# A softmax tile that is turned through memory: one fetch per tile in place of four, 128-byte sends, and products that read the tile by steps

## The chip, the cores and the metric

The kernel runs on one core of one Trainium2 chip. The metric is the device time in microseconds (us) of one execution. The core has a matrix engine (TensorE, "PE" in the profile; its weight loads are "PEld"), VectorE ("DVE"), ScalarE ("ACT"), GpSimd ("POOL") and SyncE ("SP"), which here only issues transfers. Sixteen DMA engines carry them.

## The reference

Input x is 2 batches of 1024 tokens of width 512. One attention layer and one mixture of low-rank experts are added to it:

```
def _rmsnorm(t, w):
    return t * rsqrt(mean(t * t, axis=-1) + 1e-6) * w
q = rmsnorm((LN(x) @ Wq.T) as 32 heads of 128)      # LN: layer norm without weights
k = rmsnorm((LN(x) @ Wk.T) as 8 heads of 128);  v = (LN(x) @ Wv.T) as 8 heads of 128
scores = q . k / sqrt(128) + slope[head] * (key - query), masked where key > query
attn = softmax(scores);  out = attn @ v;  x = x + out @ Wo.T
x = x + 2 * sum_h gate_h(LN(x)) * (LN(x) @ A_h.T) @ B_h.T   # gate: 8 * softmax of 8 router logits
```

Everything is float32, with 4 query heads for each of the 8 key/value heads.

## The kernel before

**Tiling.** Work goes by `w`, 16 windows: window w is one key/value head (8 of them, `NG`) of one batch. In a window the 1024 queries are 8 tiles `s` of 128 rows, the keys 8 tiles `j` of 128, and because of the mask only tiles j <= s are computed. `G = 4` query heads go together. For each (w, s): four `scores` products into PSUM (one per head h), `max` on DVE (which also moves the scores into `probs`), `exp` on ACT, `invert` on DVE, `normalise` on POOL, one instruction for each head over a row of (s+1)*128 keys. Then, for every j, the 128x128 probability blocks of the four heads have to be turned, so that keys lie on partitions, and `values` multiplies them with v into `o_ps` (128 x 512: four heads by 128 queries). `y` multiplies the result by the output weights.

**Precision.** A float32 operand is split in a high and a low part (type fp32r), and each product is three matmuls (high*high, high*low, low*high) in `split_product`; all of them have line L1106 in the profile. So one `values` is three matmuls of 128 x 512.

**Two ways to turn a tile.** A table `MEMORY_TILES` says by stage and s which j go through memory (`through_memory`). The others (260 of 576) are turned on PE: `turn.p`, four transposes, then `high` on ACT and `low` on DVE. The 316 tiles that go through memory take this way:
- `send_p` (SP, L642): once for each head, the head's normalised rows of all memory tiles of this s go to `p_bounce` in DRAM. It waits for `normalise` of that head.
- `fetch_p` (SP, L653): it waits until all four heads have landed and until the raw tile's last user (`lower_p`, L887) is done, then issues four transfers, one for each block of 32 keys. Each brings for 32 partitions sixteen pieces of 32 floats (128 bytes) for each partition. The four counts are added up in one semaphore, `p_fetched`.
- `flip_p` (DVE, L987): a transpose of every 32 x 32 block, in place. Now keys lie on partitions, and the 512 columns are (head, query).
- `upper_p` (ACT, L797) and `lower_p` (POOL, L887) split the tile in `pT_hi` and `pT_lo` (also `_a` and `_b`, further slots of early and late windows; raw tiles `p_raw`, `p_raw_b` likewise).
- `values` (PE) multiplies it, after the tiles of the same s that were turned on PE.

**Order.** The order of the work on every engine is written out by hand in the plans (`PROLOGUE`, `GROUP_A`, `BOUNDARY`, `FIRST_B`, `GROUP_B`, `LAST`); every engine takes its own items from them in order, and an item that waits holds up all that is behind it on its engine. SP's queue holds the sends, the fetches, loads of x and stores. The windows 0 to 6 are stage 0, window 7 is stage 1, and the windows 8 to 15 are stage 2. Weights are loaded, spilled and read back by transfers issued from ACT.

Of the kernel before, what the change touches and what calls it, by code (L numbers as in the profile page):

```python
# [11 lines left out]
F32 = mybir.dt.float32  # L12
# [3 lines left out]
P = 128  # L16
# [291 lines left out]
def attention_lora_block(nc, x, Wq, Wk, Wv, Wo, q_norm_w, k_norm_w, A, B, Wr, br, out):  # L308
# [4 lines left out]
    G = H // NG  # L313
    NE, RK, _ = A.shape
    NT = S // P
# [12 lines left out]
    BLOCK = 32  # L328
    NBLK = P // BLOCK
# [10 lines left out]
    def stage(w):  # L340

        return 0 if w < NG - 1 else 1 if w < NG else 2

    def through_memory(w, s):

        return list(MEMORY_TILES[stage(w)].get(s, ()))
# [4 lines left out]
    def ffn_batch(w):  # L351
        return 0 if w < LAST_W else 1
# [39 lines left out]
    raw_tile, raw_uses, raw_before = {}, {}, {}  # L392
# [41 lines left out]
    with ExitStack() as ctx:  # L434
        def sb(name, shape, dt=F32):
            return ctx.enter_context(nc.sbuf_tensor(name, shape, dt))

        def psum(name, shape):
            return ctx.enter_context(nc.psum_tensor(name, shape, F32))

        def sem(name):
            return ctx.enter_context(nc.semaphore(name))
# [12 lines left out]
        v_hi = sb("v_hi", [P, NT, HD], F32R)  # L455
        v_lo = sb("v_lo", [P, NT, HD], F32R)
        kv_raw = sb("kv_raw", [P, NT, 2 * HD])
        rel = sb("rel", [P, S])
        probs = [sb("probs_even", [P, G, S - P]), sb("probs_odd", [P, G, S])]
# [66 lines left out]
        def p_high(slot):  # L526
            return turned_pairs[slot][0]

        def p_low(slot):
            return turned_pairs[slot][1]  # L530

        def raw_p(n):
            return raws[n]


        early = [name for name in p_slot if name[0] < NG - 1]
        last_early_slots = [[name for name in early if p_slot[name] == TURN_SLOTS + MEMORY_SLOTS + i][-1] for i in range(MORE_SLOTS[0])]
# [2 lines left out]
        def ffn_place_free(engine):  # L540
            for name in last_early_slots:
                after(engine, "values", *name)
            for name in last_early_raws:
                after(engine, "lower_p", *name)

        def x_source(b, t):
            if b == 0:
                return y[:, t, :]
            return w_raw[:, (t + G) % (G + 2), :]
# [14 lines left out]
        def pairs(turned):  # L564
            return turned[:].rearrange("p (a c) n -> p a (c n)", c=2).bitcast(F32)

        p_bounce = nc.dram_tensor("p_bounce", [2, NT, G, P, P], F32).ap()

        s_ps = psum("s_ps", [P, 1024])
        turn_ps = [psum(f"turn_ps{i}", [P, 512]) for i in range(RING)]  # L570
# [1 line left out]
        o_ps = psum("o_ps", [P, 512])  # L572
# [4 lines left out]
        p_sent = [sem("p_sent_even"), sem("p_sent_odd")]  # L577
        p_fetched = [sem(f"p_fetched{i}") for i in range(RAW_TILES + sum(MORE_RAW))]
# [25 lines left out]
        def after(engine, kind, *key):  # L604
            engine.wait_ge(sems[kind], number[(kind, *key)])
# [6 lines left out]
        @block.sync  # L612
        def _(sp):
            x_v = x.rearrange("b (t p) d -> b p t d", p=P)
            out_v = out.rearrange("b (t p) d -> b p t d", p=P)

            def load_wkv(w, *first):
                if first:
                    sp.dma_start(w_raw[:, G, :], wk_v[0]).then_inc(wkv_loaded, 16)
                    sp.dma_start(w_raw[:, G + 1, :], wv_v[0]).then_inc(wkv_loaded, 16)  # L620

            def load_wq(w, *first):
                if first:
                    sp.dma_start(w_raw[:, 0:G, :], wq_v[0]).then_inc(wq_loaded, 16)

            def load_wo(w, *first):
                if first:

                    sp.dma_start(wk_norm[:], k_norm_w.rearrange("(p a) -> p a", a=1)).then_inc(small_loaded, 16)
                    sp.dma_start(wq_norm[:], q_norm_w.rearrange("(p a) -> p a", a=1)).then_inc(small_loaded, 16)  # L630
                    sp.dma_start(br_row[:], br.rearrange("(a n) -> a n", a=1).broadcast_to((P, NE))).then_inc(small_loaded, 16)
                    after(sp, "turn", "wq", 0, C - 1)
                    sp.dma_start(w_raw[:, 0:G, :], wo_v[0]).then_inc(wo_loaded, 16)

            def send_p(w, s, h):

                first = through_memory(w, s)[0]
                before = [name for name in sent if name[1] % 2 == s % 2 and sent[name] == sent[w, s] - 16 * G]
                if before and h == 0:
                    after(sp, "flip_p", *before[0], through_memory(*before[0])[-1])  # L640
                after(sp, "normalise", w, s, h)
                sp.dma_start(p_bounce[s % 2, first:s + 1, h].rearrange("u p c -> p u c"),  # L642
                             probs[s % 2][:, h, first * P:(s + 1) * P].rearrange("p (u c) -> p u c", c=P)).then_inc(p_sent[s % 2], 16)

            def fetch_p(w, s, j):

                n = raw_tile[w, s, j]
                sp.wait_ge(p_sent[s % 2], sent[w, s])
                if raw_before[w, s, j]:
                    after(sp, "lower_p", *raw_before[w, s, j])  # L650
                blocks = p_bounce[s % 2, j].rearrange("h (a i) (b j) -> b i (h a) j", i=BLOCK, j=BLOCK)
                for b in range(NBLK):
                    sp.dma_start(raw_p(n)[b * BLOCK:(b + 1) * BLOCK, :].rearrange("p (n j) -> p n j", j=BLOCK),  # L653
                                 blocks[b]).then_inc(p_fetched[n], 16)

            def load_y(w, t):
                b = 0 if w < 0 else 1
                if b:
                    sp.wait_ge(stored[t], 16)
                sp.dma_start(y[:, t, :], x_v[b, :, t, :]).then_inc(y_loaded[t], 16)  # L660

            def load_x(w, t):
                if t < 2:
                    after(sp, "turn", "wkv", NG - 1, 1)
                elif t < G + 2:
                    after(sp, "turn", "wo", NG - 1, G - 1)
                else:
                    after(sp, "turn", "x", 1, t - G - 2)
                sp.dma_start(x_source(1, t), x_v[1, :, t, :]).then_inc(x_loaded[t], 16)

            def load_a(w):
                ffn_place_free(sp)
                sp.dma_start(f_x[:, 0, :], A.rearrange("h r d -> (h r) d")).then_inc(a_loaded, 16)

            def load_wr(w):
                ffn_place_free(sp)
                sp.dma_start(f_x[0:NE, 1, :], Wr).then_inc(wr_loaded, 16)

            def load_b(w):
                after(sp, "turn", "a")  # L680
                sp.dma_start(b_raw, B.rearrange("h (p o) r -> p h o r", o=C)).then_inc(b_loaded, 16)

            def store(w, t):
                b = ffn_batch(w)
                after(sp, "add_f", b, t)
                sp.dma_start(out_v[b, :, t, :], y[:, t, :]).then_inc(stored[t], 16)

            follow({"load_wkv": load_wkv, "load_wq": load_wq, "load_wo": load_wo, "send_p": send_p, "fetch_p": fetch_p, "load_y": load_y,
                    "load_x": load_x, "load_a": load_a, "load_wr": load_wr, "load_b": load_b, "store": store})
            for t in range(NT):  # L690
                sp.wait_ge(stored[t], 16 * NB)
# [200 lines left out]
        def _(dve):  # L892
# [89 lines left out]
                                                   ALU.subtract).then_inc(sems["low"], 1)  # L982

            def flip_p(w, s, j):
                dve.wait_ge(p_fetched[raw_tile[w, s, j]], 16 * NBLK * raw_uses[w, s, j])
                raw = raw_p(raw_tile[w, s, j])
                nc.vector.transpose(raw, raw).then_inc(sems["flip_p"], 1)  # L987

# [105 lines left out]
        def _(pe):  # L1094
# [8 lines left out]
            def split_product(target, pairs, start=True, stop=True):  # L1103
                for i, ((a_hi, a_lo), (b_hi, b_lo)) in enumerate(pairs):
                    for k, (a, m) in enumerate(((a_hi, b_hi), (a_hi, b_lo), (a_lo, b_hi))):
                        last = nc.tensor.matmul(target, a, m, start=start and i == 0 and k == 0,  # L1106
                                                stop=stop and i == len(pairs) - 1 and k == 2)
                return last
# [124 lines left out]
            def values(w, s, j):  # L1233
                order = values_order(w, s)
                if j == order[0]:
                    if s == 0:
                        after(pe, "v_low", w)
                    if w or s:
                        after(pe, "o_low", w - (s == 0), (s - 1) % NT)
                r = p_slot[w, s, j]  # L1240
                if j in through_memory(w, s):
                    after(pe, "lower_p", w, s, j)
                else:
                    after(pe, "low", "p", w, s, j)
                split_product(o_ps[:], [((v_hi[:, j, :], v_lo[:, j, :]), (p_high(r), p_low(r)))],
                              start=j == order[0], stop=j == order[-1]).then_inc(sems["values"], 1)

            def y_product(w, s):
# [42 lines left out]
```

## Time and profile before

| | |
|---|---|
| median of 3 runs | 2059.68 us (2056.29 to 2061.45) |
| the profiled execution's own time | 2058.6 us |
| its span | 2056.5 us |
| PE busy | 1993.2 us, 97% |
| DVE, POOL, ACT busy | 1363.5, 1189.2, 1162.6 us |
| DMA engines, SP's queue | 41.7% of 16 engines' span |
| tiles fetched through memory | 316, by 1264 transfers of 64 KB |
| sends | 384, of 64 to 384 KB |

The span runs from the first to the last instruction; the run's own time is 2.1 us longer. Busy time of PE is the union of its matmuls, whose modelled lengths overlap: two matmuls that start 0.23 us apart may each be listed at 0.39 us. So the distance between starts, and not the listed length, is the price of a matmul in a full stream.

### The profile page before, as it was taken

How to read it: one execution, taken by the hardware profiler on the slowest of the kernel's cores; microseconds unless marked ns; L12 is line 12 of the kernel's file. 1: busy time of each engine (PE TensorE's matmuls, PEld its weight loads, DVE VectorE, ACT ScalarE, POOL GpSimd, SP SyncE). 2: the span in 40 equal slices, each digit the busy share in tenths (PEclk: the TensorE clock that was granted, in tenths of full speed). 3: DMA queues.
4: the chain of work that ended last, by engine and by line, in shares of the span. 5: the costliest groups of instructions: out<-in, count | busy, mean ns of one | idle time of the engine just before them, and what ended most of it. 6: DMA issues, size and time to landing. Idle time of an engine off the chain costs nothing.

```text
span 2056.5 us, 33589 instructions
## 1 busy us (share of the span) xinstructions
PE 1993.2 (97%) x10956; PEld 1698.1 (83%) x10956; DVE 1363.5 (66%) x3431; ACT 1162.6 (57%) x3314; POOL 1189.2 (58%) x1188
## 2 busy tenths in 40 slices
PE   7999999999999999999999899999999999999996
PEld 6888888888888888888888788787878878788774
DVE  6667667666666666768876566565666656566696
ACT  4656656565665656655555465555656555465552
POOL 3574645647465574655645557465664746657473
PEclk9999999999999999999999999999999999999998
DMA  4573855657466573765635637365463745637254
GB/s 164 138 161 119 192 141 150 132 154 166 129 171 145 136 159 113 181 181 142 135 109 141 142 96 173 96 154 139 123 124 108 172 101 137 161 81 165 69 122 99
DMA packets 896141, 283.81 MB, mean 138 GB/s; under 512 B 677721, under 2 KB 839513, under 8 KB 895969
## 3 DMA queue, kind: packets, MB, share of 16 engines
q1 hardware_dynamic: 844064, 179.44, 41.7%
q10 hardware_dynamic: 51904, 102.24, 14.2%
q8 instruction: 88, 1.44, 0.3%
q14 instruction: 85, 0.69, 0.1%
HBM read 152.59 MB, written 128.97 MB: 137 GB/s over the span
## 4 chain that ended last, share of the span: by engine, by line
PE 76%; SPq 8%; DMA 4%; DVE 4%; issue 4%; POOL 2%; ACT 2%; DVEq 0%; POOLq 0%; ACTq 0%
PE s_ps L1106 16%; PE q_ps L1106 15%; PE y_ps L1106 14%; PE o_ps L1106 14%; PE turn_ps L1193 9%; SPq L653 7%; PE turn_ps L1106 7%; DMA p_bounce<-probs_odd 2%; POOL probs_odd L881 1%; DMA p_raw_b<-p_bounce 1%; DMA p_bounce<-probs_even 1%; DVE oT_lo L1029 1%; PE turn_ps L1187 1%; SPq L642 1%; ACT oT_hi L823 1%
## 5 line engine op out<-in xcount | busy, mean ns | idle before, releaser
L881 POOL TENSOR_TENSOR probs_odd<-probs_odd,p_inv 128x256 f32<-128x256 f32 (+3 forms) x256 | 318.0, 1257 | 180.1 <-DVE p_inv L1008 179.2
L881 POOL TENSOR_TENSOR probs_even<-probs_even,p_inv 128x128 f32<-128x128 f32 (+3 forms) x256 | 261.3, 1043 | 191.3 <-DVE p_inv L1008 190.5
L1106 PE MATMUL s_ps<-kT_hi,qT_hi 128*128 128x512 f32 (+3 forms) x768 | 272.5, 355 | 4.1 <-DVE neg_max L1001 3.8
L1001 DVE CUSTOM_DVE_ANT_0 probs_odd<-s_ps,rel 128x256 f32<-128x256 f32 (+3 forms) x256 | 209.3, 820 | 97.3 <-issue 96.6
L802 ACT ACTIVATE probs_odd<-probs_odd,neg_max 128x256 f32<-128x256 f32 (+3 forms) x256 | 212.2, 831 | 91.7 <-DVE neg_max L1001 91.6
L1106 PE MATMUL s_ps<-kT_hi,qT_lo 128*128 128x512 f32 (+3 forms) x768 | 262.4, 342 | 0.0
L1106 PE MATMUL s_ps<-kT_lo,qT_hi 128*128 128x512 f32 (+3 forms) x768 | 261.7, 341 | 0.0
L802 ACT ACTIVATE probs_even<-probs_even,neg_max 128x128 f32<-128x128 f32 (+3 forms) x256 | 185.1, 725 | 118.7 <-DVE neg_max L1001 118.4
L1001 DVE CUSTOM_DVE_ANT_0 probs_even<-s_ps,rel 128x128 f32<-128x128 f32 (+3 forms) x256 | 174.9, 687 | 109.8 <-issue 108.8
L987 DVE STREAM_TRANSPOSE p_raw<-p_raw 128x512 f32<-128x512 f32 x252 | 174.9, 700 | 83.5 <-DMA p_raw<-p_bounce 83.2
L1106 PE MATMUL q_ps<-wqT_hi,xnT_hi 128*128 128x512 f32 x512 | 217.2, 424 | 1.0 <-DVE qn L1012 0.8
L1106 PE MATMUL y_ps<-woT_hi,oT_hi 128*128 128x512 f32 x512 | 204.8, 400 | 10.9 <-DVE oT_lo L1029 8.6
L789 ACT ACTIVATE pT_hi<-turn_ps 128x512 fp32r<-128x512 f32 x260 | 154.3, 597 | 107.3 <-PE turn_ps L1193 107.3
L887 POOL TENSOR_TENSOR pT_lo<-p_raw,pT_hi 128x512 fp32r<-128x512 f32 x134 | 173.8, 1301 | 49.7 <-ACT pT_hi L797 49.6
L1106 PE MATMUL q_ps<-wqT_hi,xnT_lo 128*128 128x512 f32 x512 | 201.6, 394 | 0.0
L1106 PE MATMUL y_ps<-woT_hi,oT_lo 128*128 128x512 f32 x512 | 200.5, 392 | 0.0
L1106 PE MATMUL q_ps<-wqT_lo,xnT_hi 128*128 128x512 f32 x512 | 200.4, 391 | 0.0
L1106 PE MATMUL y_ps<-woT_lo,oT_hi 128*128 128x512 f32 x512 | 199.9, 390 | 0.0
L979 DVE TENSOR_TENSOR pT_lo<-turn_ps,pT_hi 128x512 fp32r<-128x512 f32 x260 | 174.8, 677 | 27.2 <-ACT pT_hi L789 26.1
L811 ACT ACTIVATE qn<-q_ps 128x128 f32<-128x128 f32 x512 | 134.7, 280 | 94.9 <-PE q_ps L1106 93.9
L1106 PE MATMUL o_ps<-pT_hi,v_hi 128*128 128x512 f32 x426 | 177.3, 416 | 4.5 <-DVE pT_lo L979 3.7
L1106 PEld LDWEIGHTS s_ps<-kT_hi,qT_hi 128*128 128x128 f32 x768 | 144.6, 188 | 32.0 <-DVE neg_max L1001 9.1
(131 smaller groups left out, 5068.3 us busy)
## 6 DMA issues: line engine op xcount, KB each, us to landing
p_raw<-p_bounce SPq DMA_DIRECT2D x1008, 64.0 KB, 2.3
p_bounce<-probs_odd SPq DMA_DIRECT2D x60, 384.0 KB, 3.1
p_raw_b<-p_bounce SPq DMA_DIRECT2D x256, 64.0 KB, 2.4
p_bounce<-probs_odd SPq DMA_DIRECT2D x60, 256.0 KB, 2.8
p_bounce<-probs_even SPq DMA_DIRECT2D x60, 256.0 KB, 3.0
p_bounce<-probs_even SPq DMA_DIRECT2D x64, 192.0 KB, 2.4
wq_kept<-wqT_hi ACTq DMA_DIRECT2D x8, 1024.0 KB, 4.5
wq_kept<-wqT_lo ACTq DMA_DIRECT2D x8, 1024.0 KB, 6.8
```

The costliest lines, as they stand in the source:

```text
L642: sp.dma_start(p_bounce[s % 2, first:s + 1, h].rearrange("u p c -> p u c"), probs[s % 2][:, h, first * P:(s + 1) * P].rearrange("p (u c) - ...
L653: sp.dma_start(raw_p(n)[b * BLOCK:(b + 1) * BLOCK, :].rearrange("p (n j) -> p n j", j=BLOCK), blocks[b]).then_inc(p_fetched[n], 16)
L789: nc.scalar.activation(target, bank, ACT.Copy).then_inc(sems["high"], 1)
L802: nc.scalar.activation(row, row, ACT.Exp, bias=neg_max[:, s % 2, h:h + 1], scale=-1.0, accum_out=p_sum[:, s % 2, h:h + 1]).then_inc(sems[" ...
L811: last = nc.scalar.activation(qn[:, h, :], q_ps[:, h * HD:(h + 1) * HD], ACT.Square, scale=float(slopes[gg % NG * G + h]), accum_out=q_sum ...
L881: nc.gpsimd.tensor_tensor(row, row, p_inv[:, s % 2, h:h + 1].to_broadcast((P, L)), ALU.mult).then_inc(sems["normalise"], 1)
L887: nc.gpsimd.tensor_tensor(p_low(r), raw_p(raw_tile[w, s, j]), p_high(r).bitcast(F32), ALU.subtract).then_inc(sems["lower_p"], 1)
L979: nc.vector.tensor_tensor(target, bank, upper.bitcast(F32), ALU.subtract).then_inc(sems["low"], 1)
L987: nc.vector.transpose(raw, raw).then_inc(sems["flip_p"], 1)
L1001: nc.vector.tensor_tensor_reduce(out=probs[s % 2][:, h, 0:L], in0=s_ps[:, at_col:at_col + L], in1=rel[:, S - L:S], scale=-float(slopes[w % ...
L1106: last = nc.tensor.matmul(target, a, m, start=start and i == 0 and k == 0, stop=stop and i == len(pairs) - 1 and k == 2)
L1193: last = nc.tensor.transpose(bank[0:width, i * rows:(i + 1) * rows], source, ident[0:rows, 0:rows])
```

## The change

In memory, a tile is now laid out as `[head, j, block of 32 keys, query row, 32 keys]`. A send writes pieces of 32 floats (128 bytes) in place of 128 floats (512 bytes). A fetch is one transfer for all 128 partitions: partition (b, i) takes, for each head, the four query rows 4i to 4i+3 of key block b, which lie together (512 bytes). So row q is split as q = 4i + a, and not as q = 32a + i as before. After `flip_p` the columns of the tile are in the order (head, a, i), and `values` reads the tile with a step of 32 floats over a, inside steps of 1 over i, so that the product's columns come out in the order of the queries. Tiles turned on PE are read as before. `flip_p`, `upper_p` and `lower_p` work on the same 128 x 512 tiles, and all plans are the same.

```
+        def rows_in_order(tile):
+            return tile.rearrange("p (h a i) -> p h i a", h=G, a=NBLK)
...
-        p_bounce = nc.dram_tensor("p_bounce", [2, NT, G, P, P], F32).ap()
+        p_bounce = nc.dram_tensor("p_bounce", [2, G, NT, NBLK, P, BLOCK], F32).ap()
...
-                sp.dma_start(p_bounce[s % 2, first:s + 1, h].rearrange("u p c -> p u c"),
-                             probs[s % 2][:, h, first * P:(s + 1) * P].rearrange("p (u c) -> p u c", c=P)).then_inc(p_sent[s % 2], 16)
+                sp.dma_start(p_bounce[s % 2, h, first:s + 1].rearrange("u b p j -> p (u b) j"),
+                             probs[s % 2][:, h, first * P:(s + 1) * P].rearrange("p (u j) -> p u j", j=BLOCK)).then_inc(p_sent[s % 2], 16)
...
-                blocks = p_bounce[s % 2, j].rearrange("h (a i) (b j) -> b i (h a) j", i=BLOCK, j=BLOCK)
-                for b in range(NBLK):
-                    sp.dma_start(raw_p(n)[b * BLOCK:(b + 1) * BLOCK, :].rearrange("p (n j) -> p n j", j=BLOCK),
-                                 blocks[b]).then_inc(p_fetched[n], 16)
+                tile = p_bounce[s % 2, :, j].rearrange("h b (i a) j -> (b i) h (a j)", a=NBLK)
+                sp.dma_start(raw_p(n).rearrange("p (h k) -> p h k", h=G), tile).then_inc(p_fetched[n], 16)
...
-                dve.wait_ge(p_fetched[raw_tile[w, s, j]], 16 * NBLK * raw_uses[w, s, j])
+                dve.wait_ge(p_fetched[raw_tile[w, s, j]], 16 * raw_uses[w, s, j])
...
+                target, upper, lower = o_ps[:], p_high(r), p_low(r)
                 if j in through_memory(w, s):
                     after(pe, "lower_p", w, s, j)
+
+                    target = target.rearrange("p (h i a) -> p h i a", h=G, a=NBLK)
+                    upper, lower = rows_in_order(upper), rows_in_order(lower)
                 else:
                     after(pe, "low", "p", w, s, j)
-                split_product(o_ps[:], [((v_hi[:, j, :], v_lo[:, j, :]), (p_high(r), p_low(r)))],
+                split_product(target, [((v_hi[:, j, :], v_lo[:, j, :]), (upper, lower))],
                               start=j == order[0], stop=j == order[-1]).then_inc(sems["values"], 1)
```

## Rows read from the trace of the kernel before

**Rows 1.** The page: engines' busy time, and the DMA queue of SP.

```profile
PE 1993.2 (97%) x10956; PEld 1698.1 (83%) x10956; DVE 1363.5 (66%) x3431; ACT 1162.6 (57%) x3314; POOL 1189.2 (58%) x1188
...
q1 hardware_dynamic: 844064, 179.44, 41.7%
```

**Rows 2.** Windows: us, busy us of PE, PEld, DVE, ACT, POOL, clock, DMA share, GB/s.

```profile
0.00:16.00 16.00, 5.58 (x28) 4.81 (x28) 11.01 (x64) 4.91 (x8) 7.08 (x20) 1.00 0.68 230
16.00:1108.00 1092.00, 1082.01 (x6084) 929.91 (x6085) 749.32 (x1870) 642.19 (x1842) 621.99 (x632) 1.00 0.58 146
...
1856.00:2056.50 200.50, 179.70 (x908) 143.33 (x906) 142.05 (x351) 93.38 (x249) 113.11 (x110) 0.97 0.49 108
```

**Rows 3.** Waits of PE: us in total, times, longest us.

```profile
PE turn_ps L1193 <- DVE probs_odd L917: 10.1, 1, 10.1
PE o_ps L1106 <- POOL pT_lo_b L887: 9.5, 13, 1.8
```

**Rows 4.** Timeline of PE in window 9: start us, us, engine, instruction.

```profile
1393.75 0.28 PE L1106 MATMUL turn_ps<-wkvT_hi,xnT_hi 128*128 128x256 f32 x1
...
1395.18 0.28 PE L1106 MATMUL turn_ps<-wkvT_hi,xnT_hi 128*128 128x256 f32 x1
...
1403.50 0.40 PE L1106 MATMUL o_ps<-pT_hi_b,v_lo 128*128 128x512 f32 x1
...
1404.89 0.39 PE L1106 MATMUL o_ps<-pT_hi,v_lo 128*128 128x512 f32 x1
```

**Rows 5.** Copies on DVE at L944: duration ns min/median/max, starts, shape.

```profile
L944 DVE COPY f_x<-turn_ps x16: 645/682/692, 950.2 to 2045.3; 128x512 f32<-128x512 f32 x16
...
L944 DVE COPY low_turned<-turn_ps x16: 251/281/293, 967.0 to 2050.9; 128x128 f32<-128x128 f32 x16
...
L944 DVE COPY bT<-turn_ps x1: 1076/1076/1076, 944.3 to 944.3; 128x512 f32<-128x512 f32 x1
```

**Rows 6.** Issues of sends and fetches on SP's queue: issue ns min/median/max.

```profile
L653 SPq DMA_DIRECT2D p_raw<-p_bounce x1008: 302/488/2642, 67.4 to 2023.9; - x168
L653 SPq DMA_DIRECT2D p_raw_b<-p_bounce x256: 302/488/2061, 1101.2 to 2028.1; - x128
L642 SPq DMA_DIRECT2D p_bounce<-probs_even x192: 319/376/1095, 59.6 to 1993.7; - x192
```

**Rows 7.** DMA issues of the page: KB each, median us to landing.

```profile
p_raw<-p_bounce SPq DMA_DIRECT2D x1008, 64.0 KB, 2.3
p_bounce<-probs_odd SPq DMA_DIRECT2D x60, 384.0 KB, 3.1
...
p_bounce<-probs_odd SPq DMA_DIRECT2D x60, 256.0 KB, 2.8
...
p_bounce<-probs_even SPq DMA_DIRECT2D x64, 64.0 KB, 1.5
```

**Rows 8.** Timeline of SP's queue, fetches of s = 7 in window 9.

```profile
1402.82 6.29 SPq L653 DMA_DIRECT2D p_raw<-p_bounce  x12
```

**Rows 9.** DMA queue in 1402 to 1413, fetches alone: packets, MB, share.

```profile
q1 hardware_dynamic: 10781, 1.34, 76.8%
```

**Rows 10.** DMA queue in 1398 to 1400, sends alone.

```profile
q1 hardware_dynamic: 1202, 0.60, 103.2%
```

**Rows 11.** Waits of DVE and of SP's queue for those transfers: us, times, longest.

```profile
DVE p_raw L987 <- DMA p_raw<-p_bounce: 83.2, 63, 4.2
DVE p_raw_b L987 <- DMA p_raw_b<-p_bounce: 41.7, 27, 3.4
...
SPq L653 <- DMA p_bounce<-probs_odd: 116.1, 41, 8.9
SPq L653 <- DMA p_bounce<-probs_even: 112.6, 40, 8.4
```

**Rows 12.** Timeline of PE at the fifth tile of that s, with the idle time before.

```profile
1416.31 0.50 PE L1106 MATMUL o_ps<-pT_hi_b,v_hi 128*128 128x512 f32 x1 [0.87 <-POOL pT_lo_b L887]
```

**Rows 13.** Normalisation on POOL by row length: count, busy us, mean ns of one.

```profile
L881 POOL TENSOR_TENSOR probs_odd<-probs_odd,p_inv 128x1024 f32<-128x1024 f32 x64 | 121.0, 1902 | 31.2 <-DVE p_inv L1008 31.2
```

## The prediction

> **What bounds the kernel now.** I read the page's busy times first: PE is busy for 1993.2 of 2056.5 us, and no other engine for more than 1363.5 [rows 1]. Then the windows, to see where PE's 63.3 idle us lie: 10.4 in the first 16 us, 20.8 in the last 200, and only 10 in the 1092 us of the windows 0 to 7 [rows 2]. The rest, some 22 us, lies in the later windows. The granted clock is 1.00 in the full stretches, the upper of its two levels, so PE has nothing to gain there. Then PE's waits: the largest is at the start, 10.1 us, and the next, 9.5 us in 13 cases, is of `values` for `lower_p`, that is, for a tile that comes through memory [rows 3]. So the kernel is bound by PE's stream. What shortens the road through memory can return about 10 us directly; what makes a matmul longer is paid in full.
>
> The chain of waits of the page goes through SP for 8% and DMA for 4%, which looks like more. But a chain only tells the order of releases: PE was at work on other items while those transfers ran, and 3% idle is the ceiling of any gain.
>
> **What one stepped product costs.** The change makes 316 tiles times three matmuls = 948 matmuls read their moving operand by steps. In a full stream six matmuls of 512 columns start within 1404.89 - 1403.50 = 1.39 us, 0.232 each, and twelve of 256 columns within 1.43 us, 0.119 each [rows 4]. The difference, 0.1125 us for 256 columns, gives 0.225 us for the columns of one product, beside 0.007 of fixed price. So a column comes at full pace, and a slower read cannot hide behind the fixed part.
>
> No matmul of this trace reads by steps, so the price has to be bounded. Below: nothing, if reading by 128-byte steps is as fast as reading in a row. Above, the nearest row is on another engine and for a write: the one copy that goes to SBUF by steps of 16 bytes, `bT`, takes 1076 ns where the copies of the same size take 682 and those of 128 columns 281 [rows 5]. From 682 and 281, a contiguous element costs 401/384 = 1.04 ns and the fixed part is 148 ns; then a stepped one costs (1076 - 148)/512 = 1.81 ns, 1.74 times as much. Carried to PE as a ratio this is 0.74 x 0.225 = 0.167 us for each matmul, 948 x 0.167 = 158 us. Carried as a rate (an element each 1.81 ns) it is 0.928 - 0.225 = 0.70 us, 666 us in all. I take a factor of two, 0.225 x 948 = 213 us: if an array that takes a column at every step of its clock misses its operand, it loses a whole step at the least, and two is the first whole number above 1.74. It is an estimate from rows 4 and 5, and nearer to the ratio than to the rate, since one copy of DVE says more on how much a missed line costs an engine than on how fast PE's own port is.
>
> The Trainium skill has a rule that speaks against the change: "SBUF — State Buffer", section "Door 1: The DMA port swizzle (why `[64,N]` ≈ `[32,N]`)", says that SBUF is read in lines of 16 bytes, that a pattern needs two hits in a line for full bandwidth, and that each crossing to a new line pays. With steps of 128 bytes every element is in another line than the one before it. The `bT` copy agrees with it in kind, on a write and on DVE [rows 5]; no row here shows it for PE. The page gives no figure, so the sum above stands as it is.
>
> Nothing else changes on PE: the number of matmuls, weight loads and PSUM columns is the same, and the output is written in order.
>
> **The fetch.** A fetch is four issues of 488 ns at the median [rows 6]; in a stream of them twelve take 6.29 us, 0.524 each, so a tile costs SP 2.10 us [rows 8]. After it is one issue. Is an issue of more pieces longer? The sends have 128 to 768 pieces, and they are issued in 376 ns at the median, less than a fetch of 512 [rows 6]; I take 0.5 us a tile. DMA work: in the stretch with fetches alone 10781 packets take 76.8% of 16 engines for 11 us, 12.5 ns each [rows 9]; with sends alone 1202 take 103.2% for 2 us, 27.5 ns each [rows 10]. A tile is 2048 pieces of 128 bytes before, 1.60 us, and 512 of 512 bytes after, 0.88 us. So six tiles in a row (s = 7) come in about 5.3 us where they took 12.6. One transfer of 512 such pieces, 256 KB, lands in about 2.8 us, as the send of that size does [rows 7]; now the fourth of a tile's transfers is issued 1.6 us after the first and lands 2.3 later. The first tile gains 1.1 us.
>
> **The send.** Its pieces go from 512 to 128 bytes and are four times as many: 3072 for one head at s = 7. Their packet as a write to memory is in no row; from below I price it as the read of 128 bytes, 12.5 ns, from above as the 512-byte packet, 27.5 ns, and take the lower, since the two rows fit a price that goes by the bytes (one stretch reads memory, the other writes it, and neither stands out) [rows 9, 10]. The number of 128-byte packets stays 316 x 2048 = 647 thousand; they only move from fetch to send. A head takes 2.4 us where it took 1.32. POOL hands over a head each 1.90 us [rows 13], so three heads build up 3 x 0.5 us, and the last lands 1.5 + 1.1 = 2.6 us later. Queued behind it on SP are the fetches, which wait for all four heads (228.7 us of such waits in 81 cases) [rows 11]; behind the fetch `flip_p` on DVE, then ACT, POOL and `values`. At s = 7 the first tile is so late by 2.6 - 1.1 = 1.5 us, and the sixth early by 7.3 - 2.6 = 4.7.
>
> That sixth is where it counts: the stream of tiles is what PE waits for there, 0.87 us before the fifth [rows 12], while the first tile stands behind two tiles that were turned on PE. DVE also stands less in `flip_p`, where it now waits 124.9 us in 90 cases [rows 11]. What PE can get back is its own waits: 9.5 us [rows 3], perhaps as much again out of waits behind a delayed DVE. I take -10 us, between 0 and -25. The same 10 us fall away if PE is slowed instead, as its producers then have more time: they are counted once.
>
> **The sum** for the likeliest case, against the profiled execution's own 2058.6 us: 2058.6 + 213 - 10 = 2262 us. That execution is 1 us under the median of the runs, 2059.68, which changes nothing.
>
> **The rivals.**
> - *The stepped read is free* (the other sign). Place: the 948 matmuls of `values`. For it: the steps are regular, and only the order of addresses changes. Against: `bT` [rows 5]. Then what is left is the shorter road: 2058.6 - 10 = 2049 us, 2034 to 2059 by the bounds. It decides below a price of 10/948 = 0.011 us for a matmul, 5% of its columns.
> - *The read is far slower*, at the rate of `bT`, 1.81 ns an element: 2058.6 + 666 - 10 = 2715 us. For it: if the price is a latency of the memory and not of the engine, it is the same time for everyone. Against: DVE's contiguous element takes 1.04 ns, PE's 0.44, so the two ports have not the same pace to begin with.
> - *The sends become the bound*, with a free read. At 27.5 ns a piece a head of s = 7 takes 5.3 us against POOL's 1.90; the last lands 3 x 3.4 + 4.0 = 14 us later, and the fetches give back 7.3. At s = 5 and 6 (four tiles) it is some 3 us each after what the fetches give back. That is 13 us a window, 208 us over 16 windows, of which I take half to be covered by other PE work: 2058.6 + 104 = 2163 us. It starts to lose at 4 x (192 p - 1.9) = 7.3 us, p = 19 ns a packet. The Trainium skill, "DMA: Bandwidth & Descriptors", section "Specifications", says that below 512 bytes the engine does a read-modify-write; no row here shows it for a write, and the 128-byte reads of rows 9 show no such price.
> - *The change does not do what it says*: a transfer of 128-byte pieces might hold SP for longer, so that the three issues saved come back in the sends. Against it is that issue time does not grow with the pieces [rows 6]. With it the gain is gone, and nothing more: 2059 with a free read.
>
> **How the numbers follow.** Read slowed about twofold, 2262 (own range 2206 to 2290: the ratio of 1.74 without more, and the factor two with nothing gained): 0.45. Read free: 0.33, of which 0.20 is faster by over 0.3% (6 us, about what a measurement of this kernel can tell from no change) and 0.13 within it. Far slower: 0.12. Sends the bound: 0.05. The rest, 0.05, is some small loss of another kind. The range goes from 2040, which takes in most of the free case, to 2300; it leaves out the far slower read and a few of the others, 0.19. Faster 0.20, same 0.14, slower 0.66.
>
> **What the profile of the changed kernel would show.** If I am right, the matmuls of `values` come in two kinds: those of tiles turned on PE start 0.23 us apart, those of fetched ones about 0.45; PE's busy time grows by some 200 us, `flip_p` no longer waits for DMA, and PE's wait for `pT_lo_b` is gone. If both kinds start 0.23 apart, the read is free, and the result is decided on the road through memory: by the landing time of the sends (2.5 to 3.1 us now at 256 to 384 KB; I expect about 5 at 384 KB), and by SP's queue at s = 7, one issue a tile. A landing of over 10 us would be the rival of the sends. Wrong the forecast would be above all if the moving operand's port does not care for lines.

## The result and the profile after

The changed kernel is slower by 0.6%: 2070.52 us (median of 4 runs, 2069.65 to 2071.27) against 2058.27 us of the kernel before, ratio 1.0062, 95% interval 1.0049 to 1.0074. I had forecast slower, and 2262 us: right in sign and in the direction of the mechanism, but 203 us of loss where 12 came, because one term, the price of the stepped read, was five times too large.

The page of the kernel after, with the lines that answer to [rows 1] and [rows 7]:

```profile
span 2069.2 us, 32641 instructions
...
PE 2024.2 (98%) x10956; PEld 1701.7 (82%) x10956; DVE 1356.6 (66%) x3431; ACT 1162.1 (56%) x3314; POOL 1193.7 (58%) x1188
...
q1 hardware_dynamic: 828896, 179.38, 43.3%
...
p_raw<-p_bounce SPq DMA_DIRECT2D x252, 256.0 KB, 3.3
p_bounce<-probs_odd SPq DMA_DIRECT2D x60, 384.0 KB, 4.8
```

PE is busy for 31.0 us more (2024.2 against 1993.2) and idle for 45.0 us in place of 63.3. So PE's own work grew by more than the whole loss, and some of its waits are gone. A fetch is one transfer, in the air for 3.3 us; a send of 384 KB lands after 4.8 us where it took 3.1.

The timeline of PE after, in window 9 (start us, us, instruction), to be read beside [rows 4]:

```profile
1417.12 0.39 PE L1107 MATMUL o_ps<-pT_hi,v_lo 128*128 128x512 f32 x1
1417.35 0.39 PE L1107 MATMUL o_ps<-pT_hi,v_hi 128*128 128x512 f32 x1
1417.58 0.39 PE L1107 MATMUL o_ps<-pT_lo,v_hi 128*128 128x512 f32 x1
1417.80 0.39 PE L1107 MATMUL o_ps<-pT_hi,v_lo 128*128 128x512 f32 x1
1418.03 0.43 PE L1107 MATMUL o_ps<-pT_hi_b,v_hi 128*128 128x512 f32 x1
1418.30 0.43 PE L1107 MATMUL o_ps<-pT_lo_b,v_hi 128*128 128x512 f32 x1
1418.57 0.43 PE L1107 MATMUL o_ps<-pT_hi_b,v_lo 128*128 128x512 f32 x1
```

The first four belong to tiles turned on PE and start 0.23 us apart. The last three read a fetched tile by steps and start 0.27 apart. So there are two kinds, as forecast, but the step costs 0.27 - 0.23 = 0.04 us and not 0.225; over 948 matmuls some 40 us and not 213. (The listed lengths overlap, so it is the distance between starts that counts.)

The waits of PE after (us in total, times, longest):

```profile
PE turn_ps L1194 <- DVE probs_odd L918: 10.0, 1, 10.0
...
PE y_ps L1107 <- DVE oT_lo L1030: 4.5, 8, 0.7
...
PE o_ps L1107 <- DVE pT_lo L980: 0.5, 1, 0.5
```

The 9.5 us for `pT_lo_b` of [rows 3] have no successor: no product waits any longer for a fetched tile. DVE's waits for fetched tiles fell from 124.9 us [rows 11] to 49.9; I had expected them to be gone:

```profile
DVE p_raw L988 <- DMA p_raw<-p_bounce: 39.7, 30, 3.4
...
DVE p_raw_b L988 <- DMA p_raw_b<-p_bounce: 10.2, 8, 2.0
```

### The profile page after: what moved, and what is told of

Same layout as the page of the kernel before. It is cut to its first block, busy times and chain, and to the rows that moved or that the text cites. A ratio compares the mean times of both kernels' runs of the same rounds, so it can differ in the third digit from the quotient of the medians.

```text
span 2069.2 us, 32641 instructions
## 1 busy us (share of the span) xinstructions
PE 2024.2 (98%) x10956; PEld 1701.7 (82%) x10956; DVE 1356.6 (66%) x3431; ACT 1162.1 (56%) x3314; POOL 1193.7 (58%) x1188
## 4 chain that ended last, share of the span: by engine, by line
PE 92%; DVE 3%; issue 1%; ACT 1%; POOL 1%; DMA 1%; SPq 0%; DVEq 0%; POOLq 0%; ACTq 0%
PE o_ps L1107 20%; PE s_ps L1107 18%; PE y_ps L1107 17%; PE q_ps L1107 17%; PE turn_ps L1194 11%; PE turn_ps L1107 8%; PE turn_ps L1188 1%; PE y_ps L1271 0%; DVE qn L1013 0%; DVE oT_lo L1030 0%; DMA p_raw_b<-p_bounce 0%; ACT oT_hi L824 0%; DVE y L1036 0%; ACT qn L812 0%; DMA y<-in_L_attn_x 0%
## 5 line engine op out<-in xcount | busy, mean ns | idle before, releaser
L1107 PE MATMUL o_ps<-pT_hi,v_hi 128*128 128x512 f32 x426 | 183.7, 431 | 0.8 <-DVE pT_lo L980 0.5
L1107 PE MATMUL o_ps<-pT_hi,v_lo 128*128 128x512 f32 x426 | 174.6, 410 | 0.0
```

## The experiments

**The two halves by themselves.** The theory after the result: the stepped read costs some 40 us (A), and the shorter road gives part of it back. The rival (B): the loss is the sends' small pieces. First the read alone, in the kernel before:

```
 # the kernel before, and in values (rows_in_order as in the change):
+                target, upper, lower = o_ps[:], p_high(r), p_low(r)
...
+                    target = target.rearrange("p (h i a) -> p h i a", h=G, a=NBLK)
+                    upper, lower = rows_in_order(upper), rows_in_order(lower)
```

> The kernel before, its memory layout, sends and fetches untouched; only the 948 products of fetched tiles read the turned tile by the steps of the change. (The columns of the four heads come out in another query order, so the values of the output differ.) Theory A, the loss of the change is the price of the stepped read and the shorter road gives part of it back: these matmuls start 0.27 us apart in place of 0.23, PE's busy time grows by some 40 us, and the time is 2058 + 41 less what PE's waits for producers give back (up to 13): 2085 to 2100 us, clearly above the 2070.5 of the whole change. Theory B, the stepped read costs little where producers are late anyway, and the loss comes from the sends of 128-byte pieces: 2058 to 2065 us.

Measured: 2080.66 us against 2056.66, ratio 1.0114 (1.0101 to 1.0128), 24.0 us slower. It came out just below the range, and far above what B allows. By form, the products of fetched tiles before and, below them, in that run (count, busy us, mean ns of one):

```profile
L1106 PE MATMUL o_ps<-pT_lo_b,v_hi 128*128 128x512 f32 x80 | 31.7, 396 | 0.0
...
L1106 PE MATMUL o_ps<-pT_lo_a,v_hi 128*128 128x512 f32 x70 | 27.6, 395 | 0.0
```

```profile
L1109 PE MATMUL o_ps<-pT_lo_b,v_hi 128*128 128x512 f32 x80 | 35.0, 438 | 0.0
...
L1109 PE MATMUL o_ps<-pT_lo_a,v_hi 128*128 128x512 f32 x70 | 30.5, 436 | 0.0
```

Each is 0.041 to 0.042 us longer, some 40 us for 948. Of these, 24 reach the end: most of the rest falls into time in which PE stood idle anyway (63.3 us before, 50.0 here). Then the road alone, the whole change with the read put back:

```
 # the kernel after, and in values:
-                    target = target.rearrange("p (h i a) -> p h i a", h=G, a=NBLK)
-                    upper, lower = rows_in_order(upper), rows_in_order(lower)
```

> The whole change, but the products read the fetched tiles in a row. (The columns are then in another query order, so the values of the output differ.) Theory A: the road through memory is faster than before, PE gets back its waits for fetched tiles, and the time falls below before: 2030 to 2052 us, with PE busy time as before, 1993. Theory B, the small pieces of the sends are the loss: 2062 to 2070 us, with PE waiting for pT_lo more than the 9.5 us of before.

Measured: 2039.91 us, ratio 0.9918 (0.9904 to 0.9931), 16.7 us faster. A is right, B falls. The two halves add up to +7.3 us, the whole change was +12.3: with the shorter road there is less idle time left for the slower products to hide in. PE's idle time shows it: the read alone takes 13.3 us of the 63.3 away, the road alone 14.2 (49.1 are left), and both together only 18.3 (45.0 are left). They are two effects of opposite sign, of which the change keeps the difference.

**What on the road gives the gain.** Four transfers of 512-byte pieces in place of one, in the improved kernel told below (2038 us), so the pieces of sends and fetches are the same in both:

```
 # the kernel with two stored identities, and in fetch_p:
-                tile = p_bounce[s % 2, :, j].rearrange("h b (i a) j -> (b i) h (a j)", a=NBLK)
-                sp.dma_start(raw_p(n).rearrange("p (h k) -> p h k", h=G), tile).then_inc(p_fetched[n], 16)
+                for b in range(NBLK):
+                    tile = p_bounce[s % 2, :, j, b].rearrange("h (i a) j -> i h (a j)", a=NBLK)
+                    sp.dma_start(raw_p(n)[b * BLOCK:(b + 1) * BLOCK, :].rearrange("p (h k) -> p h k", h=G),
+                                 tile).then_inc(p_fetched[n], 16)
```

> The run with two identity tiles, but a tile is again fetched by four transfers of 32 partitions each, now of 512-byte pieces (the sends stay at 128 bytes). The output is the reference's. Theory A: the gain on the road through memory is that of SP's queue (2.1 us a tile by four issues of 0.52): with four issues back, the time returns from 2038 to about 2055 or above, since the sends still land 1 to 1.7 us later. Theory B: it is the DMA engines' work (0.9 us a tile in place of 1.6), and four issues of larger pieces keep most of it: 2038 to 2045 us.

Measured: 2106.70 us, ratio 1.0247 (1.023 to 1.0263). It went A's way, but no theory saw the size: the three further issues of a tile cost 68 us, and bring the kernel 50 us over the kernel before, which has as many. SP's queue at s = 7 of window 9, with four issues and with one:

```profile
1424.10 1.75 SPq L664 DMA_DIRECT2D p_raw_b<-p_bounce  x4
1425.94 5.59 SPq L664 DMA_DIRECT2D p_raw<-p_bounce  x12
1431.64 3.71 SPq L664 DMA_DIRECT2D p_raw_b<-p_bounce  x8
```

```profile
1394.82 0.36 SPq L663 DMA_DIRECT2D p_raw_b<-p_bounce  x1
1395.28 1.55 SPq L663 DMA_DIRECT2D p_raw<-p_bounce  x3
1397.17 4.11 SPq L663 DMA_DIRECT2D p_raw_b<-p_bounce  x2
```

24 issues take 11.3 us, six take 6.5. Of the six, five go out within 3.1 us, and the last stands 3.0 us for its raw tile, which `lower_p` still reads. The pieces of a fetch are larger than before, and yet with four issues SP needs 0.47 us for each (0.52 before [rows 8]): a tile is then paced by the issues, not by the bytes. The late sends (4.2 us to landing at 384 KB, where the kernel before has 3.1), which one issue a tile pays for, are here without cover. DVE stands in `flip_p` for 184.3 us where the kernel before has 124.9 [rows 11], and PE waits for DVE's other work behind it (waits of DVE and of PE in the run with four issues):

```profile
DVE p_raw L1003 <- DMA p_raw<-p_bounce: 121.2, 82, 4.8
...
DVE p_raw_b L1003 <- DMA p_raw_b<-p_bounce: 63.1, 28, 4.4
...
PE o_ps L1122 <- DVE pT_lo L995: 20.4, 7, 5.3
PE y_ps L1122 <- DVE oT_lo L1045: 15.0, 14, 2.7
```

Behind them the clock falls as well; window of the same run: PE busy for 9.79 of 12 us, granted clock 0.86. Over the whole run the granted clock is 0.989 in place of 0.997, and PE's busy time 17.5 us above that of the kernel before.

```profile
1424.00:1436.00 12.00, 9.79 (x40) 7.65 (x39) 6.25 (x9) 4.09 (x7) 5.32 (x4) 0.86 0.44 125
```

So with four issues a tile the new layout (sends in 128-byte pieces, fetches in 512-byte ones) loses some 50 us against the old one, the fallen clock included. Of its two sides the fetches land sooner (2.0 us in place of 2.3) and the sends later, so I put the loss on the sends; small sends with the old fetches were not run. What the change gives by one issue in place of four is 68, in this kernel and with these sends.

**Why the step is cheap.** I had expected a factor of two. Three probes on the kernel before, each with another order of reading the fetched tiles; nothing else differs:

```
 p1: tile.rearrange("p (h i a) -> p h a i", h=G, a=4)   # steps of 4 floats, runs of 32
 p2: tile.rearrange("p (x y a) -> p y x a", a=4, x=8)   # 4 floats in a row, then 64 on
 p3: tile.rearrange("p (h i a) -> p h a i", h=G, a=2)   # steps of 2 floats, runs of 64
```

> The kernel before; the products of fetched tiles read steps of 4 floats (16 bytes) in runs of 32. (Columns in another order, so the output's values differ.) If the price is for each element in another 16-byte line, these matmuls are as slow as with steps of 32 floats, 0.437 us each by the profile, against 0.396 in a row. If it is for each restart of the inner run (128 restarts with steps of 32, 16 here), about 0.401. If it is for the distance of 128 bytes, 0.396.

> The kernel before; the products of fetched tiles read runs of 4 floats in a row (16 bytes), each run 32 floats behind the one before it. (Columns in another order, so the output's values differ.) Price for elements in another line: a run is one line, as in a row, 0.396 us. Price for restarts: 128 as in the change, 0.437 us.

> The kernel before; the products of fetched tiles read steps of 2 floats (8 bytes) in runs of 64, two elements for each line of 16 bytes. (Columns in another order, so the output's values differ.) If two elements a line are enough for full pace, 0.396 us; if the price grows with the lines for each element, half of the price of 16-byte steps, about 0.41; if for restarts (8 of them), 0.398.

(In p2 the next run starts 64 floats further on, and not 32 as its expectation says: with x = 8, y has 16 values, and a step of x is 16 x 4 floats. It has 128 runs of 4 all the same.)

Measured, one execution each: 2247.14, 2082.64 and 2238.81 us. The middle one costs about what the change's order costs. The other two cost a factor of two for each product, and come within 15 and 23 us of the 2262 that I had forecast. Three consecutive starts of p1, p2 and p3, from their timelines of PE:

```profile
1420.14 0.66 PE L1109 MATMUL o_ps<-pT_hi_b,v_hi 128*128 128x512 f32 x1
1420.60 0.66 PE L1109 MATMUL o_ps<-pT_lo_b,v_hi 128*128 128x512 f32 x1
1421.06 0.66 PE L1109 MATMUL o_ps<-pT_hi_b,v_lo 128*128 128x512 f32 x1
```

```profile
1424.18 0.44 PE L1109 MATMUL o_ps<-pT_hi_b,v_hi 128*128 128x512 f32 x1
1424.45 0.45 PE L1109 MATMUL o_ps<-pT_lo_b,v_hi 128*128 128x512 f32 x1
1424.73 0.46 PE L1109 MATMUL o_ps<-pT_hi_b,v_lo 128*128 128x512 f32 x1
```

```profile
1494.42 0.63 PE L1109 MATMUL o_ps<-pT_lo_b,v_hi 128*128 128x512 f32 x1
1494.87 0.63 PE L1109 MATMUL o_ps<-pT_hi_b,v_lo 128*128 128x512 f32 x1
1495.33 0.63 PE L1109 MATMUL o_ps<-pT_hi,v_hi 128*128 128x512 f32 x1
```

0.46, 0.27 to 0.28 and 0.45 us apart. For p1 and p3 all theories fall: none allowed more than 0.04 us over a read in a row, and these take 0.22 and more. A price for each element in another line falls also because the change's own order changes line with every element, too, and costs 0.27. Only for p2 did a theory's number come, that of the 128 restarts. So what was open is why the change's order is cheap and p1's is not: the distance of 128 bytes, the short run of 4, or that the change returns to the same four lines with the next run. Three more probes tell these apart:

```
 q1: tile.rearrange("p (g a y) -> p g y a", a=4, y=4)   # steps of 4, runs of 4, each line again after 4 columns
 q2: tile.rearrange("p (a i) -> p i a", a=16)           # steps of 32, runs of 16, each line again after 16
 q3: tile.rearrange("p (a x y) -> p y x a", a=4, y=4)   # steps of 128, runs of 4, each line again after 128
```

> The kernel before; the products of fetched tiles read steps of 4 floats in runs of 4, four such runs within 16 floats, so that every 16-byte line is touched again after three others. (Columns in another order, so the output's values differ.) If what makes the change's read cheap is the distance of 128 bytes, this one costs what steps of 4 floats in runs of 32 did: 0.46 us from start to start. If it is the short run, or that a line is touched again soon, 0.27.

> The kernel before; the products of fetched tiles read steps of 32 floats in one run of 16 over the whole tile, then the next column. (Columns in another order, so the output's values differ.) Distance decides: 0.24 to 0.27 us, with 32 restarts in place of 128. The short run or an early return to the same line decides: 0.46.

> The kernel before; the products of fetched tiles read steps of 128 floats in runs of 4, and the next run starts 4 floats on, so that no 16-byte line is touched again before 128 columns. (Columns in another order, so the output's values differ.) If the run of 4 alone makes the read cheap: 0.27 us. If it is the early return to the same lines: 0.46.

Measured, one execution each: 2079.78, 2222.71 and 2270.69 us. Starts of q1, q2 and q3:

```profile
1421.37 0.43 PE L1109 MATMUL o_ps<-pT_hi_b,v_hi 128*128 128x512 f32 x1
1421.63 0.43 PE L1109 MATMUL o_ps<-pT_lo_b,v_hi 128*128 128x512 f32 x1
1421.90 0.43 PE L1109 MATMUL o_ps<-pT_hi_b,v_lo 128*128 128x512 f32 x1
```

```profile
1500.45 0.61 PE L1109 MATMUL o_ps<-pT_lo_b,v_hi 128*128 128x512 f32 x1
1500.88 0.61 PE L1109 MATMUL o_ps<-pT_hi_b,v_lo 128*128 128x512 f32 x1
1501.31 0.61 PE L1109 MATMUL o_ps<-pT_hi_b,v_hi 128*128 128x512 f32 x1
```

```profile
1416.73 0.65 PE L1109 MATMUL o_ps<-pT_hi_b,v_hi 128*128 128x512 f32 x1
1417.20 0.67 PE L1109 MATMUL o_ps<-pT_lo_b,v_hi 128*128 128x512 f32 x1
1417.69 0.66 PE L1109 MATMUL o_ps<-pT_hi_b,v_lo 128*128 128x512 f32 x1
```

0.27, 0.43 and 0.48 us. Distance is not it: 16 bytes (q1) is as cheap as 128. A short run is not it: q3 has runs of 4 and is the dearest. The theory of the early return said what each of the three would do before they ran, and all three came out about so. It holds in all seven orders: where four neighbouring floats (16 bytes, called a line here) are used one after the other or with a return after 4 columns (the change, p2, q1), a matmul costs 0.27 to 0.28; where a part of a line is used now and another 16 or more columns later (q2, q3, p1, and p3, which uses two floats at a time), 0.43 to 0.48. A return after 5 to 15 columns was not tried. That such lines are held for a moment is inferred from these seven; how many, and for how long, was not tried.

Two things stay open. The first is the size of the line. p3 uses two floats of each 16 bytes in succession, so it changes line half as often as p1, and yet costs as much (0.45 against 0.46). With a unit of 8 bytes it would use one float of each at a time, as p1 does, and all seven orders would fit as well; pairs of floats in a row, with jumps between them, would decide and were not run. The second is the 0.04 us itself. The early return tells the cheap orders from the dear ones, but not a cheap one from a read in a row: p2 uses each line whole and at once, and still pays it. The three cheap orders have 128 short runs each, so a small price for each restart, 0.3 ns, would give it; a price for each jump does not fit, since the change jumps 512 times and p2 128 times. Cheap orders with fewer or more restarts were not run.

**Where else the step can be put.** The two engines that split the tile can put its rows in order:

```
-                nc.scalar.activation(p_high(...), raw_p(...), ACT.Copy)
+                nc.scalar.activation(in_rows(p_high(...)), rows_in_order(raw_p(...)), ACT.Copy)
...
-                nc.gpsimd.tensor_tensor(p_low(r), raw_p(...), p_high(r).bitcast(F32), ALU.subtract)
+                nc.gpsimd.tensor_tensor(in_rows(p_low(r)), rows_in_order(raw_p(...)), in_rows(p_high(r)).bitcast(F32), ALU.subtract)
```

> The whole change, but the order of the rows is put right one step earlier: upper_p on ScalarE and lower_p on GpSimd read the raw tile by the steps of 32 floats and write in a row, and the products read in a row. The output is the reference's. Theory A, a stepped read costs any engine something, and here it falls on engines that are busy for 56 to 58%: upper_p goes from 0.63 to 0.7 to 1.3 us, lower_p from 1.3 to at most 2.6; if it is under 0.3 us each it is hidden and the time is that of the run with the road alone, 2030 to 2052; at a doubling, lower_p holds GpSimd for another 400 us in the windows where it is already the pace of the last tiles, and the time is 2070 to 2150. Theory B (the sends are the loss): not below 2062 in any case.

Measured: 2064.10 us, ratio 1.0037 (1.0025 to 1.005). Better than the change, not better than before, and between A's two ranges. B's "not below 2062" is met too; it is the run with the road alone that excludes B, not this one. The two instructions, before and in this run (count, busy us, mean ns of one):

```profile
L887 POOL TENSOR_TENSOR pT_lo<-p_raw,pT_hi 128x512 fp32r<-128x512 f32 x134 | 173.8, 1301 | 49.7 <-ACT pT_hi L797 49.6
...
L797 ACT ACTIVATE pT_hi<-p_raw 128x512 fp32r<-128x512 f32 x134 | 84.1, 628 | 59.5 <-DVE p_raw L987 55.1 <-PE o_ps L1106 4.1
```

```profile
L891 POOL TENSOR_TENSOR pT_lo<-p_raw,pT_hi 128x512 fp32r<-128x512 f32 x134 | 213.1, 1597 | 51.6 <-ACT pT_hi L801 51.1
...
L801 ACT ACTIVATE pT_hi<-p_raw 128x512 fp32r<-128x512 f32 x134 | 156.2, 1172 | 49.1 <-DVE p_raw L991 47.0
```

The same order of reading that costs PE 18% costs ScalarE 87%: it falls on the chain from the landed tile to the product, 0.54 + 0.30 us a tile, and this run is 24 us above the road alone. PE waits 11.9 us here for the low parts that POOL makes, and not at all in the run with the road alone.

**No step at all.** If partition 4i+a of the scores holds query 32a+i, the fetched tile comes out in the natural order by itself. A turn on PE should permute for nothing if the identity that it multiplies with has its columns permuted; the mask table is permuted once, through memory:

```
+        eye_p = sb("eye_p", [P, P])    # ident, read "p (i a) -> p a i" once
...
-                    last = nc.tensor.transpose(bank[...], source, ident[0:rows, 0:rows])
+                    eye = eye_p[:] if of == "p" else ident[:].rearrange("p (a i) -> p i a", a=NBLK) if of == "q" else ident[0:rows, 0:rows]
+                    last = nc.tensor.transpose(bank[...], source, eye)
...
+                    sp.dma_start(rel_kept, rel[:]).then_inc(rel_sent, 16)
+                    sp.wait_ge(rel_sent, 16)
+                    sp.dma_start(rel[:], rel_kept.rearrange("(a i) n -> i a n", a=NBLK)).then_inc(rel_back, 16)
```

> The whole change with no stepped product at all and the reference's output: the query tile is turned against an identity whose columns are permuted, so that partition 4i+a of the scores holds query 32a+i, the mask table is permuted alike through memory once at the start, and tiles turned on TensorE use the inverse permuted identity. The only stepped reads left are the 512 of the small query turns (128 columns each). Theory A: the time of the road alone plus at most 5 us: 2033 to 2055, below before. Theory B: 2062 to 2072.

Measured: 2095.29 us, ratio 1.0189 (1.0175 to 1.0203), 40 us above A's range and 23 above B's. Its timeline of PE has the reason: four turns with the stored identity, and four that read it by steps.

```profile
1217.70 0.60 PE L1208 MATMUL turn_ps<-eye_p,probs_even 128*128 128x128 f32 x4
1218.83 1.05 PE L1208 MATMUL turn_ps<-ident,qn 128*128 128x128 f32 x4
```

0.45 us more for four turns, 0.11 each, over 512 turns 58 us. I had allowed 5, from the price in `values`. These are turns of plain float32, not of fp32r, and there the same order of reading (steps of 32 floats, runs of 4) doubles the time, from 0.11 to 0.22 us from start to start. With a second stored identity, for which keeping one `low_gated` tile in place of two makes room:

```
-        eye_p = sb("eye_p", [P, P])
+        eyes = {"p": sb("eye_p", [P, P]), "q": sb("eye_q", [P, P])}
...
-        low_gated = sb("low_gated", [P, 2, P])
+        low_gated = sb("low_gated", [P, 1, P])
```

> As the run with turned queries, but the query turns read a second identity tile, stored with its columns already in the wanted order, in a row and not by steps (room for it comes from keeping one low_gated tile in place of two). The output is the reference's. Theory A (a stepped moving operand has a price on TensorE and all else of the change is a gain): the query turns go back from 0.40 to 0.27 us each, 512 x 0.12 = 63 us less than 2095, and the time is that of the road alone, 2035 to 2047 us, below both kernels. Rival: the loss of the run with turned queries came from elsewhere (the mask's way through memory, the permuted identities), and it stays above 2070.

Measured: 2038.17 us against 2055.79, ratio 0.9915 (0.9901 to 0.9928), and it computes what the reference does. It beats both kernels, by 0.85% that before, and has the time of the road alone: the permutation costs nothing that can be measured.

## Why the prediction was wrong

- **What bounds the kernel.** Right. PE's stream sets the end; of the 40 us by which the read alone lengthens PE's work 24 were paid, so "paid in full" was too much, and a change of the road moved little but PE's waits.
- **The stepped product** is the step that failed: "I take a factor of two, 0.225 x 948 = 213 us". It measured 0.04 x 948 = some 40 us. The mechanism, a moving operand that is slower to read by steps, was right, and the term was mis-sized by five. The 2070.5 lies inside the range of 2040 to 2300, but by luck: the case I gave the largest chance, 2206 to 2290, did not come, and the range reached so far down only to take in a free read. What came is nearest to the "small loss of another kind", at 0.05. I sized it by the write of `bT` [rows 5], which goes by steps of 16 bytes over the whole tile and so is near to the order of p1 and not to that of the change; p1 did cost the factor of two. What I had not weighed is that the inner run of 4 comes back to the same lines with the next step of 1. The Trainium skill's rule of 16-byte lines and two hits in each ("SBUF — State Buffer", section "Door 1: The DMA port swizzle (why `[64,N]` ≈ `[32,N]`)") does not hold for this operand as it stands: p3 takes two floats of each 16 bytes in turn and still costs 0.45 us where a row costs 0.23. The runs agree with it in that it matters when the neighbours of a float are used; that the line has 16 bytes they do not show.
- **The fetch.** 0.5 us an issue taken, 0.36 to 0.46 us measured at the median; 2.8 us to landing taken, 3.3 measured. Six tiles of s = 7 were to come in 5.3 us in place of 12.6; their issues take 6.5, 3.0 of it the wait for a raw tile.
- **The send.** About 5 us to landing forecast at 384 KB, 4.8 measured. While sends ran almost alone in the run after, 2744 packets took 127.7% of 16 engines for 2 us, 14.9 ns each, against the 12.5 that I took and the 27.5 of the upper bound (first the queue in those 2 us, then all issues of sends after, as in [rows 6]):

```profile
q1 hardware_dynamic: 2744, 0.37, 127.7%
```

```profile
L645 SPq DMA_DIRECT2D p_bounce<-probs_even x192: 359/360/4347, 59.5 to 2005.2; - x192
L645 SPq DMA_DIRECT2D p_bounce<-probs_odd x192: 359/360/5107, 69.2 to 2023.7; - x192
```

- **Whether sends hold SP for longer** was my last rival, and I had set it aside because issue time does not grow with the pieces. At the median it does not: 360 ns where it was 376. But the longest took 1.1 us for the even s [rows 6] and 1.5 for the odd ones, and now take 4.3 and 5.1, and the issues of all 384 sends add up to 223 us in place of 163. The saving on the fetches, 643 to 183 us, is far larger, so this rival did not come either; it took an eighth of what was saved.
- **What PE gets back.** -10 taken, with 0 to -25 as bounds; the road alone gave -16.7. That is within the bounds. To count the same idle time once for the road and the slower read was right in kind, since the two do share it; but 10 us was too little for both together: of the 40 us of the read only 12.3 came out, so some 28 came back, 24.0 - 12.3 = 11.7 of them by the road.
- **The sum** with the two measured terms is 2058.6 + 40 - 17 = 2082 at most, and 2070.5 with what the idle time hid. The range of the likeliest case had a slip as well: its upper end was to be the factor two with nothing gained, and that is 2058.6 + 213 = 2272, not 2290. The measured price of 0.04 us for a matmul is above the 0.011 at which I had put the turn from faster to slower, and so the sign was right.
- **The sends as the bound** did not come, though the run with four fetches speaks for a real cost: some 50 us, hidden because the same edit took three issues in four from SP. I had priced the sends and SP's issues one by one, and missed that either alone is worth far more than the sum of both.

## What to carry to other kernels

Where one engine is busy for 97% of the time, look at what an edit adds to each of its instructions before what it saves on the road to it: 0.04 us times 948 matmuls outweighed a road with 1264 - 316 = 948 transfers fewer. For an operand that is read out of order, ask how soon its neighbours are used, not how far the step is; and where an identity matrix is multiplied anyway, a permuted one, stored, does the reordering for nothing. A transfer's pieces and the number of issues should be costed together: a loss of some 50 us and a gain of 68 look small in their sum.

## What the runs showed of the hardware

- A matmul of 128 x 512 in fp32r costs 0.23 us from start to start if its moving operand is read in a row, 0.27 if it is read by steps but four neighbouring floats are used at most 4 columns apart (the change, q1), 0.28 for four floats in a row and then a jump (p2), and 0.43 to 0.48 if neighbours are used 16 columns or more apart (q2, p3, p1, q3).
- In plain float32 a turn of 128 columns goes from 0.11 to 0.22 us for the order that costs fp32r 18%.
- The same order of reading costs ScalarE 87% (628 to 1172 ns) and GpSimd's subtraction 23% (1301 to 1597 ns) on 128 x 512.
- A fetch of 64 KB in 128 pieces of 512 bytes takes SP's queue 0.47 us an issue in a stream; in 512 pieces of 128 bytes it was 0.52. The median issue is nearly the same for any transfer here, but single issues of sends of 128-byte pieces last up to 5.1 us.
- Sent to memory in 128-byte pieces, a packet took 14.9 ns of a DMA engine, not far over the 12.5 ns of the 128-byte reads [rows 9]. For a byte that is 2.2 times the price of the 512-byte packet, 27.5 ns [rows 10].
